# An attention and feed-forward layer on one core: late modulations moved ahead of the first scores, a bias product summed on VectorE, and row statistics laid between other work

## The reference, cut to what matters

```python
mod = (silu(c) @ wmod).reshape(2, 6, 1, 256)
sa, ca, ga, sb, cb, gb = (mod[:, j] for j in range(6))
ga, gb = push_away_from_zero(ga), push_away_from_zero(gb)   # magnitude at least 0.25
h = layernorm(x) * (1 + ca) + sa
q = rotary((h @ Wq + bq) * scale); k = rotary(h @ Wk + bk); v = h @ Wv + bv     # 16 heads
attn = softmax(causal(q @ k.T)) @ v
x = x + ga * (attn @ Wo + bo)
h = layernorm(x) * (1 + cb) + sb
x = x + gb * ffn(h)                                          # silu(gate) * up, then down
```

## Time and profile before

| what | value |
|---|---|
| median of 3 runs | 1056.35 us (1055.84 to 1058.07) |
| profiled execution, its own time | 1054.73 us |
| its span, first to last instruction | 1052.6 us |
| mean granted clock of PE | 0.988 of full speed |
| PE busy | 1013.3 us, 96% of the span |
| DVE busy | 775.9 us, 74% |
| ACT busy | 679.2 us, 65% |
| POOL busy | 618.0 us, 59% |

### The profile page before, as it was taken

How to read it: one execution, slowest core, us unless ns; L and a number is a source line. 1 busy time by engine, 2 the same in 40 slices (tenths; PEclk the granted TensorE clock), 3 DMA queues, 4 the chain that set the end, 5 groups by cost and what they waited for, 6 DMA issues and landing times.

```text
span 1052.6 us, 20462 instructions
## 1 busy us (share of the span) xinstructions
PE 1013.3 (96%) x6312; PEld 909.7 (86%) x6312; DVE 775.9 (74%) x1688; ACT 679.2 (65%) x1445; POOL 618.0 (59%) x469
## 2 busy tenths in 40 slices
PE   6889999999999999999999999999999999997977
PEld 5779998999999999999989999999899999886766
DVE  6657777777777877787777777777777777887443
ACT  5756666666666666666666666676666667766642
POOL 3356755566665755575556656665656565553653
PEclk9899999999999999999999999999999999999989
DMA  6512211122112211211122111221121132111001
GB/s 201 165 31 62 51 42 41 46 55 50 30 41 70 50 40 38 63 42 38 40 71 47 39 34 32 69 50 40 41 70 43 37 85 71 41 41 41 18 23 42
DMA packets 41988, 56.03 MB, mean 53 GB/s; under 512 B 5509, under 2 KB 25029, under 8 KB 41925
## 3 DMA queue, kind: packets, MB, share of 16 engines
q1 hardware_dynamic: 41924, 55.37, 20.4%
HBM read 19.69 MB, written 2.10 MB: 21 GB/s over the span
## 4 chain that ended last, share of the span: by engine, by line
PE 89%; DVE 4%; ACT 3%; issue 2%; POOL 1%; DMA 1%; SPq 0%; DVEq 0%; ACTq 0%; POOLq 0%
PE ps_r L1329 18%; PE ps_r L1328 18%; PE ps_r L1327 17%; PE ps_t L1498 12%; PE ps_s L1329 6%; PE ps_s L1328 6%; PE ps_s L1327 6%; PE ps_s L1334 1%; PE ps_s L1337 1%; PE ps_r L1434 1%; PE ps_r L1336 1%; PE ps_r L1334 1%; DVE ps_s L1226 1%; ACT xn L926 0%; DMA wmod_a<-in_L_wmod 0%
## 5 line engine op out<-in xcount | busy, mean ns | idle before, releaser
L649 POOL TENSOR_TENSOR swapped<-swapped,sin_sb 128x512 f32<-128x512 f32 x124 | 165.9, 1338 | 242.3 <-DMA swapped<-straight 242.0
L881 ACT ACTIVATE pT_hi<-ps_t 128x512 fp32r<-128x512 f32 (+3 forms) x384 | 187.0, 491 | 86.2 <-PE ps_t L1498 84.1
L1169 DVE TENSOR_TENSOR pT_lo<-ps_t,pT_hi 128x512 fp32r<-128x512 f32 (+3 forms) x384 | 201.8, 549 | 50.9 <-ACT pT_hi L881 50.7
L1226 DVE CUSTOM_DVE_ANT_0 ps_s<-ps_s,mask_wide 128x128 f32<-128x128 f32 (+7 forms) x256 | 194.3, 759 | 55.8 <-PE ps_s L1329 41.4
L659 POOL TENSOR_TENSOR qk_lo<-straight,qk_hi 128x512 fp32r<-128x512 f32 x124 | 162.1, 1320 | 112.1 <-ACT qk_hi L788 112.1
L892 ACT ACTIVATE probs<-ps_s,neg_max 128x128 f32<-128x128 f32 (+7 forms) x256 | 190.2, 743 | 39.6 <-DVE neg_max L1226 37.3
L1498 PE MATMUL ps_t<-ident,probs 128*128 128x128 f32 x1152 | 186.0, 275 | 4.6 <-DVE pT_lo L1169 4.6
L650 POOL TENSOR_TENSOR straight<-straight,cos_sb 128x512 f32<-128x512 f32 x124 | 181.4, 1463 | 0.0
L1097 DVE TENSOR_TENSOR straight<-straight,swapped 128x512 f32<-128x512 f32 x126 | 127.2, 1010 | 32.1 <-POOL straight L650 31.9
L1498 PEld LDWEIGHTS ps_t<-ident,probs 128*128 128x128 f32 x1152 | 134.8, 140 | 8.8 <-issue 3.8
L1327 PE MATMUL ps_s<-qk_hi 128*128 128x512 f32 (+3 forms) x384 | 140.5, 366 | 1.1 <-DVE qk_lo L1123 1.1
(11 more groups left out here) (193 smaller groups left out, 2229.3 us busy)
## 6 DMA issues: line engine op xcount, KB each, us to landing
swapped<-straight SPq DMA_DIRECT2D x252, 128.0 KB, 2.2
x_in<-in_L_attn_x SPq DMA_DIRECT2D x4, 512.0 KB, 5.3
w_raw<-in_L_attn_Wk SPq DMA_DIRECT2D x8, 256.0 KB, 3.2
w_raw<-in_L_attn_Wq SPq DMA_DIRECT2D x8, 256.0 KB, 3.5
w_raw<-in_L_attn_Wv SPq DMA_DIRECT2D x8, 256.0 KB, 3.6
wo_all<-in_L_attn_Wo SPq DMA_DIRECT2D x1, 2048.0 KB, 12.3
wo_raw<-in_L_attn_Wo SPq DMA_DIRECT2D x8, 256.0 KB, 2.7
x<-in_L_attn_x SPq DMA_DIRECT2D x4, 512.0 KB, 3.9
```

The lines of the kernel that those rows point to most:

```text
L649: pool.tensor_tensor(swapped[:, q, :], swapped[:, q, :], sin_sb[:, cs], ALU.mult)
L881: nc.scalar.activation(turned_at(ORDER[step], k0, k1)(pT_hi), ps_t[:, (T_FIRST[step] + j) % 2, 0:(k1 - k0) * P].rearrange("p (k q) -> p k ...
L1169: nc.vector.tensor_tensor(turned_at(t, k0, k1)(pT_lo), ps_t[:, (T_FIRST[step] + j) % 2, 0:(k1 - k0) * P].rearrange("p (k q) -> p k q", q=P ...
L1226: nc.vector.tensor_tensor_reduce(rows, rows, mask_wide[:, SEQ - n_keys:SEQ], -1.0, -MASKED, ALU.add, ALU.min, accum_out=neg_max[:, t:t + 1 ...
```

## The change

The late modulations leave the pieces of unit 0. PE makes them in `late_mods`, ahead of `scores:0`, in a part of the score banks, and ACT copies them out in `late_mods_out`, between the last two pairs of `whiten`. Their transfers and those of the scale rows are issued right behind the first load of `Wv`, instead of behind the swaps of the first four query and key pieces. `scores:1` now waits for that copy.

The bias product is first summed over the heads by DVE: 16 instructions in a chain, four each in `bias:0` to `bias:3`, give `bias_parts[p, n]`, the sum over heads h of `bv[h, p] * Wo[h, p, n]`. PE then needs one float32 matmul with ones to sum over the 128 partitions. `make:B` moves from before `scores:5` to before `make:V0`, and `sum:B` and `gates:0` move to the back of the unit on DVE.

In the prologue DVE takes the first statistics of batch 1 (`bn_stats`) in two groups of four ahead of `h_low` 0 and 2 instead of behind `h_low` 3, and makes the low part of `V1` of the prologue (`FIRST_V[1]`) before `cosine(1)` instead of behind it. On DVE `max:1` comes ahead of `xlow:4` and `xlow:5`, and `low:V1` ahead of `add:Q1+`. The two waits on PE before the loop go.

```diff
 PLANS_0 = {
-    TENSOR_PLAN: """make:P0- make:P1- scores:0 xn:4 make:K0+ xn:5 scores:1 make:Q0+ xn:6 xn:7 make:M scores:2 turn:0.0
-        scores:3 turn:1.0 make:K1+ turn:1.1 scores:4 turn:2.0 make:B scores:5 make:Q1+ turn:3.0 turn:3.1 make:V0
+    TENSOR_PLAN: """make:P0- make:P1- mods:1 scores:0 xn:4 make:K0+ xn:5 scores:1 make:Q0+ xn:6 xn:7 scores:2 turn:0.0
+        scores:3 turn:1.0 make:K1+ turn:1.1 scores:4 turn:2.0 scores:5 make:Q1+ turn:3.0 turn:3.1 make:B make:V0
         turn:4.0 scores:6 make:V1 turn:5.0 scores:7 turn:5.1""",
-    SCALAR_PLAN: """exp:0 out:K0+ xout:4 xout:5 exp:1 out:Q0+ xout:6 xout:7 out:M exp:2 turn:0.0
+    SCALAR_PLAN: """exp:0 out:K0+ xout:4 xout:5 exp:1 out:Q0+ xout:6 xout:7 exp:2 turn:0.0
         high:K0+ turn:1.0 exp:3 high:Q0+ turn:1.1 out:K1+ turn:2.0 exp:4 out:Q1+ turn:3.0
         exp:5 turn:3.1 turn:4.0 high:V0 high:K1+ high:V1 turn:5.0 exp:6 split:O turn:5.1 high:Q1+""",
-    VECTOR_PLAN: """max:0 xlow:4 xlow:5 max:1 xlow:6 xlow:7 add:K0+ max:2 turn:0.0 add:Q0+ max:3
-        turn:1.0 turn:1.1 gates:0 max:4 turn:2.0 sum:B max:5 turn:3.0 add:K1+ turn:3.1
-        turn:4.0 max:6 low:V0 add:Q1+ low:V1 max:7 turn:5.0 turn:5.1""",
+    VECTOR_PLAN: """max:0 max:1 xlow:4 xlow:5 bias:0 add:K0+ xlow:6 xlow:7 max:2 turn:0.0 add:Q0+ max:3
+        bias:1 turn:1.0 turn:1.1 bias:2 max:4 turn:2.0 max:5 bias:3 turn:3.0 add:K1+ turn:3.1 sum:B
+        turn:4.0 max:6 low:V0 low:V1 add:Q1+ max:7 turn:5.0 turn:5.1 gates:0""",
...
@@ def _(sp):
             load_w(WV, 0)
+            load_mod(2, 3, wmod_b_ready)
+            load_mod(3, 4, wmod_b_ready)
+            for j, part in enumerate((2, 5)):
+                sp.dma_start(wmod_g[:, :, j, :], wmod_t[:, :, part, :]).then_inc(wmod_b_ready, 16)
+            sp.wait_ge(zeroed, 2)
...
             for piece in FIRST_QK:
                 swap_halves(Span(0, 0), piece)
-            load_mod(2, 3, wmod_b_ready)
-            load_mod(3, 4, wmod_b_ready)
...
@@ def _(pool):
             pool.memset(s_rows[:, :], 0.0).then_inc(zeroed, 1)
+            pool.memset(ones[:, :], 1.0).then_inc(zeroed, 1)
...
@@ def _(act):
+            def late_mods_out():
+                act.wait_ge(mod_made, 2)
+                col_out(COL_SG, SROWS, 3, ps_s[:, 1, CH:2 * CH])
+                mod_out(1, ps_s[:, 1, CH + MODS_AT:2 * CH])
...
             v_high(first, ("v", 0, 3))
+            late_mods_out()
             whiten(14)
...
@@ def _(dve):
+            late = slice(NTT // 2, NTT)
             for n in range(GROUPS4 // 2):
+                if n in (0, 2):
+                    dve.wait_ge(x_ready[2 + n // 2], 16)
+                    for t in range(NTT // 2 + 2 * n, NTT // 2 + 2 * n + 4):
+                        last = nc.vector.bn_stats(bn[:, t, :], x_in[:, t, :])
                 h_low(n)
-            late = slice(NTT // 2, NTT)
-            moments(x_in, range(NTT // 2, NTT), lambda n: dve.wait_ge(x_ready[n], 16))
+            spreads(last, range(NTT // 2, NTT))
...
             qk_add(first, FIRST_QK[0])
+            v_low(first, FIRST_V[1])
             cosine(1)
-            v_low(first, FIRST_V[1])
             qk_add(first, FIRST_QK[1])
...
+            def bias_part(n):
+
+                if n == 0:
+                    dve.wait_ge(wo_all_ready, 32)
+                    dve.wait_ge(cols_ready, 2)
+                for h in range(4 * n, 4 * n + 4):
+                    column = cols[:, COL_BV + h:COL_BV + h + 1]
+                    if h == 0:
+                        ins = nc.vector.tensor_scalar(bias_parts[:, :], wo_all[:, h, :], column, None, ALU.mult)
+                    else:
+                        ins = nc.vector.scalar_tensor_tensor(bias_parts[:, :], wo_all[:, h, :], column, bias_parts[:, :],
+                                                             ALU.mult, ALU.add)
+                    if h < HEADS - 1:
+                        link(ins)
+                    else:
+                        ins.then_inc(bias_parts_ready, 1)
...
@@ def _(pe):
-                elif piece[0] == "mods":
-                    pe.wait_ge(s_rows_ready, 80)
-                    turn_rows(s_rows, SROWS, dst[:, 0:SROWS])
-                    pe.wait_ge(wmod_b_ready, 64)
-                    ins = modulation(1, dst[:, MODS_AT:CH])
                 elif piece[0] == "bias":
-                    pe.wait_ge(wo_all_ready, 32)
-                    for h in range(HEADS):
-                        ins = nc.tensor.matmul(dst[:, 0:DIM], cols[:, COL_BV + h:COL_BV + h + 1].broadcast_to([P, P]),
-                                               wo_all[:, h, :], start=h == 0, stop=h == HEADS - 1)
+                    pe.wait_ge(zeroed, 2)
+                    pe.wait_ge(bias_parts_ready, 1)
+                    ins = nc.tensor.matmul(dst[:, 0:DIM], ones[:, :].broadcast_to([P, P]), bias_parts[:, :], start=True, stop=True)
...
-                    pe.wait_ge(mod_ready, 1)
+                    pe.wait_ge(mod_ready, 2)
...
+            def late_mods():
+                pe.wait_ge(mod_ready, 1)
+                pe.wait_ge(s_rows_ready, 80)
+                turn_rows(s_rows, SROWS, ps_s[:, 1, CH:CH + SROWS])
+                pe.wait_ge(wmod_b_ready, 64)
+                modulation(1, ps_s[:, 1, CH + MODS_AT:2 * CH]).then_inc(mod_made, 1)
...
             run(Span(0, 1))
             pe.wait_ge(hT_ready, GROUPS4)
-
-            pe.wait_ge(v_ready, sum(piece[0] == "v" for piece in BEFORE_LOOP))
-            pe.wait_ge(straight_ready, sum(piece[0] == "qk" for piece in BEFORE_LOOP))
             with pe.Fori(0, LAST) as i:
```

More of the change, by code:

```diff
@@ L168, in unit_plan @@
                 out.append((what, which, n))
-        elif name[0] in "LDHXMB":
-            kind = {"L": "late", "D": "down", "H": "h", "X": "width", "M": "mods", "B": "bias"}[name[0]]
+        elif name[0] in "LDHXB":
+            kind = {"L": "late", "D": "down", "H": "h", "X": "width", "B": "bias"}[name[0]]
             out.append((what, v, (kind, int(name[1:] or 0))))
         elif what in ("float", "largest", "moments", "newton", "normal", "ffn", "silu", "gu", "xn", "xout", "xlow",
-                      "gates", "bias"):
+                      "gates", "bias", "mods"):
             out.append((what, v, (int(name),)))
@@ L202 @@
 RANK = {piece: sum(other[0] == piece[0] for other in PIECES[:n]) for piece, n in PIECE_AT.items()}
-PER_PASS = {"qk": 4 * UNITS, "v": 2 * UNITS, "pv": 2 * UNITS, "wo": 4 * UNITS, "gate": 0, "mods": 0, "bias": 0, "late": 0, "down": 0, "h": 0, "width": 0}
+PER_PASS = {"qk": 4 * UNITS, "v": 2 * UNITS, "pv": 2 * UNITS, "wo": 4 * UNITS, "gate": 0, "bias": 0, "late": 0, "down": 0, "h": 0, "width": 0}
 PIECES_PER_PASS = sum(PER_PASS.values())
@@ L376, in build @@
         wide = small("wide", [1, 1], I32)
+        ones = small("ones", [P, 1], F32)
         assert base + small_at[0] <= nc.sbuf_usable_end, (base + small_at[0], nc.sbuf_usable_end)
@@ L411, in build @@
         attn_bias_ready = sem("attn_bias_ready")
+        bias_parts_ready = sem("bias_parts_ready")
         pool_chain = sem("pool_chain")
@@ L548, in _ @@
             load_w(WV, 0)
+            load_mod(2, 3, wmod_b_ready)
[3 more added lines that the diff above has]
+            sp.wait_ge(zeroed, 2)
+            for src, r0 in ((s_gate, 0), (s_up, HM)):
+                sp.dma_start(s_rows[r0:r0 + HM - 1, :], src[0:(HM - 1) * P].rearrange("(m p) -> m p", p=P))\
+                    .then_inc(s_rows_ready, 16)
+                sp.dma_start(s_rows[r0 + HM - 1:r0 + HM, 0:HLAST],
+                             src[(HM - 1) * P:HID].rearrange("(a p) -> a p", a=1)).then_inc(s_rows_ready, 16)
+            sp.dma_start(s_rows[2 * HM:SROWS, :], s_down.rearrange("(k p) -> k p", p=P)).then_inc(s_rows_ready, 16)
             def swap_halves(ps, piece):
@@ L989, in do @@
                 elif what == "out":
-                    {"qk": qk_out, "gate": gate_out, "late": late_out, "down": down_out, "h": h_piece_out,
-                     "mods": mods_out}[piece[0]](ps, piece)
+                    {"qk": qk_out, "gate": gate_out, "late": late_out, "down": down_out, "h": h_piece_out}[piece[0]](ps, piece)
                 else:
@@ L1038, in moments, with spreads @@
                     last = nc.vector.bn_stats(bn[:, t, :], src[:, t, :])
+                spreads(last, tiles)
+            def spreads(last, tiles):
                 link(last)
@@ L1284, in do @@
                     gate_columns()
+                elif what == "bias":
+                    bias_part(*piece)
                 else:
@@ L1552, in do @@
                     scores(ps, x, *piece)
+                elif what == "mods":
+                    late_mods()
                 elif what == "turn":
```

3 lines of the change are left out of this document (1 added, 2 removed).

## The result

The changed kernel takes 1062.78 us (median of 6 runs, 1061.65 to 1064.08) against 1056.65 us for the kernel before (six runs, 1054.75 to 1058.69). The ratio is 1.0056 with a 95% interval of 1.004 to 1.0073, so it is slower, by some 6 us. The forecast was 1053.6 us, range 1049.5 to 1057.8, with 0.12 on slower. The profiled execution took 1061.81 us with a span of 1060.0 us.

A forecast was written before the change was run, and what follows sets the result against it. PE bounds the loop, so its start on K0 of unit 1 decides, with DVE setting the pace in unit 0: 2.5 us from waits and low:V1's order plus 0.2 from the rest gives 1053.6 us, range 1049.5 to 1057.8.

The forecast's parts named there:

- Step 1: Prologue: V1's low part comes earlier, P1's gap is half a microsecond instead of 2.28 us, clock stays up.
- Step 2: Late modulations after P1: no transfer wait, 4.2 us, scores:1 ends near 40.2; PE then stands from 43.2 to 46.6.
- Step 3: Bias sum in unit 0: PE's 6.9 us become about 0.4; DVE pays 7.9 us plus collisions with POOL.
- the sum: DVE's unit 0 total: 23.4 us plus five or six collisions of about 1.1 us; K0 at 70.7, 2.7 us sooner.
- my rivals: Against the forecast: few collisions, 1049.7 us (0.22); only the waits move, 1056.3 (0.17); slower by the clock, 1059.3 (0.11).
- the slow rival: PE's longer standing in unit 0 halves the clock during V0 to turn:5.1; 3 us slower, 1059.3 us; chance 0.11.

The follow-up runs named there:

- gap_old_prologue: Changed kernel, gates:0 after max:0, bias product as 16 PE matmuls in the xout:7 gap, but DVE's prologue as in the kernel before; 1050.24 us, ratio 0.994.
- gates_back: Changed kernel with gates:0 back in its old place behind turn:1.1 on DVE; 1053.03 us, ratio 0.9976 to the kernel before.
- gates_early: Changed kernel with gates:0 moved between max:0 and max:1 on DVE; 1053.84 us, ratio 0.9974 to the kernel before.
- before_gates_late: Kernel before with only gates:0 moved to the end of DVE's list of unit 0; 1057.63 us, ratio 1.0014.
- copy_twice: Changed kernel with POOL's copy to y made twice, the second waiting for the first; 1061.84 us, ratio 1.0048 to the kernel before.
- copy_sooner: Changed kernel with POOL's copy to y taken before low:K1+ instead of after low:Q1+; 1055.74 us, ratio 0.9987 to the kernel before.
- before_gates_late_2: before_gates_late run once more for a second profile, same change to the kernel before; 1059.53 us, ratio 1.0014.
- gates_early_copy_twice: gates_early with POOL's copy to y made twice, as control for copy_twice; 1056.4 us, ratio 1.0011 to the kernel before.
- gap_waits: Changed kernel, gates:0 after max:0, bias product as 16 PE matmuls in the xout:7 gap, two PE waits before the loop restored; 1049.01 us, ratio 0.9931.

## Why the prediction was wrong, by its steps

**Step 1, the prologue: right, too small.** P1's wait fell from 2.28 to 0.63 us, P1 began at 28.64 (29.4 forecast), and the clock stayed at 1.00 from 28 to 32 us. I cost the effect on the end at next to nothing; gap_old_prologue gives it 2 to 3 us in a kernel that is not held elsewhere.

**Step 2, the late modulations: right in kind, with a wrong sum.** No DMA wait, and the first swap of K0 took 2.95 us from the end of ACT's `straight` (40.42) to POOL's start (43.37), 3 forecast. They took 30.42 to 35.7 us, 5.3 and not 4.2. The clock fell near 32.6 us, some two microseconds in, just as I had taken it; the 4.2 was badly added, since my own rows gave 1.81 + 3.37 = 5.2 for the same instructions with the same fall. That P1 began 0.8 us sooner than forecast hid most of this error. `scores:1` ended near 41.4 and not 40.2. The standing of 3.42 us for `xout:7` is as forecast.

**Step 3, the bias sum: right, with its sum.** The form that the trace of before did not show, by its group in the changed kernel:

```profile
L1174 DVE SCALAR_TENSOR_TENSOR bias_parts<-wo_all,cols,bias_parts 128x256 f32<-128x256 f32 x15 | 9.5, 632 | 0.4
```

With POOL idle four of them take 2.06 us, 0.52 each with the link, close to the 0.50 taken; the mean of 632 ns holds the collisions. Judged by their durations, five of DVE's instructions waited for POOL from 43.9 to 65.4 us, three of them in the bias sum, where five or six were forecast. `bias:3` ended at 65.37 (64.4 forecast), V0 began at 65.84 (64.8) and K0 at 71.49 (70.7).

**The step that failed** is in two sentences of the sum: "DVE and POOL stand about one and a half to two microseconds deeper behind PE in unit 1 (gates, and POOL's copy to y). I cost that at nothing, covered by the idle time that DVE has there; uncovered, up to 1." I had priced the gates at 1.0 us by their old place, from 56.8 to 57.8 us of the kernel before, where POOL was idle but for the first 0.2 us, and did not apply to them what I had worked out for the bias sum in the step before, that a DVE instruction with both inputs in SBUF waits out a POOL instruction. The traces add that four or eight columns wait as long as 512 do. In their new place POOL had 7.2 us of work in stock behind the end of a low part, and they paid for all of it. They took 7.9 us. The cover was 2.09 us in the kernel before and 1.20 in gates_back; `max:0` came 6.5 us later behind K0 than before, and 5.4 of that reached PE. With it came 2.3 us more from the clock (5.76 at the loop, +1.95, -5.39). None of my rivals held this; the slow rival's cause, the clock during V0 to `turn:5.1`, did not occur (1.00 from 66 to 74 us). The clock fell later, behind the gates' wait; in gates_back, without that wait, the windows from 78 to 90 us read 1.00. gates_back and gates_early show the cause: one word moved in one list takes 8 to 9 us off by the ratios, and nothing else of the change is touched.

The Trainium skill, "SBUF — State Buffer", section "Who interferes with whom", also counts one-input copies and `tensor_scalar` among the operations that can take the shared pair, where they can use two ports. The trace agrees: the `TENSOR_SCALAR` of four columns took 3.20 us in before_gates_late.

Open: why before_gates_late escapes the loss in half of its runs, and what the second copy of copy_twice costs in time.

## What to carry to other kernels

Price a moved instruction by what its neighbours do in the new place, not by its length in the old one: a chain of tiny VectorE instructions can cost up to one GpSimd instruction a link, for as long as GpSimd has the next one ready. Before giving PE's work to another engine, look for a place in PE's own list where it stands for others; 6.9 us of matmuls moved from their old place into a 3.4 us gap gave 4.1 us here by the ratios (and the whole kernel with them is 9 us faster than the one before), and the same work given to VectorE gave nothing that shows. And when a list in order sets the pace, follow every edit one unit further than the first point where the gain is in hand.

## What was not expected of the hardware

`TENSOR_SCALAR` with one input of four or eight columns waited for POOL as the two-input forms did (0.95, 1.19 and 3.20 us against 0.16). A semaphore in front isn't what decides. `sign` has none, nor has the `magnitude` behind it: `sign` started within 0.03 us of POOL's instruction and took 0.16 us, `magnitude` started 0.05 to 0.08 us after it and was held (3.35 us in the changed kernel, 1.26 in before_gates_late, 1.23 in copy_sooner). And two gates with a semaphore in front weren't held, because POOL was between instructions (78.67 us in copy_twice) or had none left (81.67 us in before_gates_late). In the statistics of one input (line 1098 of the changed kernel) beside POOL nothing of the kind shows: four took 1.41 us beside a POOL instruction and 1.40 with POOL idle.

The same instructions of the modulations took from 3.7 us (gates_back, gates_early) to 5.3 us (the changed kernel), by when the granted clock fell.

Executions of one kernel differ by up to 9.5 us (1055.18 to 1064.65 in before_gates_late_2), which is more than any single edit here moved a ratio. The profiles show one place where this arises. From the first load of the feed-forward part to the end all kernels have the same code, and it took from 192.65 us (gates_early_copy_twice) to 196.93 us (gap_waits). The number of PE instructions is the same there (1026), and so is the longest wait (5.3 us), but PE is busy for 169.84 us in the first and for 173.83 us in the second, and the mean granted clock is 0.97 and 0.95. For the first 96 us or so the two run alike; then comes a stretch of 12 us with the clock at 0.68 in gap_waits (945.67 to 957.67 us) and at 0.95 in gates_early_copy_twice (955.75 to 967.75 us). So up to 4 us of the difference between two executions can come in code that no edit touches, and the granted clock goes with it. Where the rest comes from isn't shown.
